# Moving a GpSimd share of the attention-to-FFN transition to VectorE, with a shorter bisection step

## What is computed

```python
x = x + jnp.tanh(g_xattn[0]) * _L0_xattn_ref(_layernorm(x), ctx_1024, ...)   # ends with gru_cell
x = x + jnp.tanh(g_ffn[0]) * _L0_ffn_ref(_layernorm(x), ...)

def _L0_ffn_ref(x, ...):
    scores = jax.nn.sigmoid(h @ gate_w.T)                     # 4096 x 16
    topk_score, topk_ids = jax.lax.top_k(scores.T, cap)       # 512 tokens for each of 16 experts
    xin = h[topk_ids]
    eo = jax.nn.silu(xin @ gw + gb) * (xin @ up + up_b)
    eo = eo @ down + down_b
    out = zeros.at[topk_ids].add(eo * topk_score)
    shared = (jax.nn.silu(x @ sh_gate_w.T) * (x @ sh_up_w.T)) @ sh_down_w.T
    return out + shared
```

## Time and profile before

| | us |
|---|---|
| median of three runs (lowest, highest) | 1204.84 (1204.55, 1205.53) |
| the profiled execution: its time | 1202.21 |
| the profiled execution: its span | 1200.5 |
| PE busy | 1114.3 (93%) |
| DVE busy | 820.7 (68%) |
| ACT busy | 559.2 (47%) |
| POOL busy | 436.6 (36%) |

### The profile page before, as it was taken

One profiled execution on the slowest core, in us unless ns is written; L12 is line 12 of the kernel. 1 busy time (PEld: TensorE's weight loads), 2 busy tenths in 40 slices (PEclk: granted clock), 3 DMA queues, 4 the chain that ended last, 5 costly groups with the idle time before them and its releaser, 6 DMA issues. The chain is left out here.

```text
span 1200.5 us, 18388 instructions
## 1 busy us (share of the span) xinstructions
PE 1114.3 (93%) x6174; PEld 964.1 (80%) x6174; DVE 820.7 (68%) x1552; ACT 559.2 (47%) x839; POOL 436.6 (36%) x334
## 2 busy tenths in 40 slices
PE   5659999999999787999988999999999999999996
PEld 3548888888888566888876888888888888888896
DVE  7575878787865986778864666566666665666663
ACT  4243545544546466232334554455555544555542
POOL 5232444344411733343541232243323423343332
PEclk9659999999999899999998999999999999999999
DMA  4310011010104234001045434454444334544421
GB/s 158 97 36 1 3 34 25 11 35 0 35 1 127 67 106 133 22 17 35 18 143 178 117 96 127 136 141 94 125 133 135 96 123 140 141 95 124 133 37 18
DMA packets 47525, 98.75 MB, mean 82 GB/s; under 512 B 11392, under 2 KB 37248, under 8 KB 43136
## 3 DMA queue, kind: packets, MB, share of 16 engines
q1 hardware_dynamic: 33728, 79.13, 20.4%
q0 software_dynamic: 12288, 17.31, 8.5%
q10 hardware_dynamic: 1472, 1.84, 0.4%
HBM read 74.11 MB, written 17.07 MB: 76 GB/s over the span
## 5 line engine op out<-in xcount | busy, mean ns | idle before, releaser
L2067 DVE SCALAR_TENSOR_TENSOR hid<-wide,b_up,silu 128x512 f32<-128x512 f32 x120 | 90.1, 751 | 165.8 <-PE wide L1317 159.4
L956 POOL DMA_INDIRECT out_tokens<-y,idx_out x64 | 111.8, 1747 | 235.2 <-DVE y L2049 188.7
L1317 PE MATMUL wide<-xt_hi,w_hi 128*128 128x512 f32 x480 | 189.3, 394 | 3.1 <-DVE xt_lo L2032 3.1
L1317 PE MATMUL wide<-xt_lo,w_hi 128*128 128x512 f32 x480 | 188.6, 393 | 0.0
L1317 PE MATMUL wide<-xt_hi,w_lo 128*128 128x512 f32 x480 | 187.6, 391 | 0.0
L1619 ACT ACTIVATE silu<-wide,b_gate 128x512 f32<-128x512 f32 x120 | 82.1, 685 | 147.8 <-PE wide L1317 147.8
L1331 PE MATMUL down<-w_hi,hid_hi 128*128 128x256 f32 x480 | 136.6, 284 | 0.0
L1331 PE MATMUL down<-w_lo,hid_hi 128*128 128x256 f32 x480 | 135.9, 283 | 0.0
L1331 PE MATMUL down<-w_hi,hid_lo 128*128 128x256 f32 x480 | 135.7, 283 | 0.0
L1628 ACT ACTIVATE hid_hi<-hid 128x512 fp32r<-128x512 f32 x120 | 76.0, 633 | 101.1 <-DVE hid L2067 101.1
L2017 DVE TENSOR_TENSOR w_lo<-raw,w_hi 128x768 fp32r<-128x768 f32 x128 | 121.4, 949 | 0.0
(11 more groups left out here) (320 smaller groups left out, 2516.2 us busy)
## 6 DMA issues: line engine op xcount, KB each, us to landing
raw<-in_w_expert SPq DMA_DIRECT2D x32, 1536.0 KB, 6.7
work<-in_x SPq DMA_DIRECT2D x8, 512.0 KB, 4.7
token_rows<-work SPq DMA_DIRECT2D x8, 512.0 KB, 3.2
out_tokens<-y SPq DMA_DIRECT2D x8, 512.0 KB, 3.0
attn<-rms_c SPq DMA_DIRECT2D x24, 128.0 KB, 2.3
attn<-expo SPq DMA_DIRECT2D x24, 128.0 KB, 2.4
b_down<-in_down_b SPq DMA_DIRECT2D x1, 2048.0 KB, 12.5
sh_full<-in_w_shared SPq DMA_DIRECT2D x1, 1536.0 KB, 6.1
```

Source lines behind the costliest of these rows:

```text
L956: pool.indirect_dma_start(out, bass.IndirectOffsetOnAxis(idx_out[:, j:j + 1], 0), y[:, j, :], None, compute_op=ALU.add).then_inc(g_add, 16)
L1317: last = nc.tensor.matmul(bank[:, f % 2, :], w[f // HALF_F][:, f % HALF_F, (c + k) * P:(c + k + 1) * P], x_[:, k, :], start=(m == 1), stop ...
L2067: nc.vector.scalar_tensor_tensor(hid[:, f % 2, :], eup[:, f % 2, :], b_up[:, bass.ds(e, 1), f:f + 1].rearrange("p a b -> p (a b)"), silu[: ...
```

## The change

1. VectorE adds x for all groups straight out of PSUM. `copy_x` on ScalarE and `add_x` on GpSimd go.
2. `h_full` goes: `high` on ScalarE rounds straight from PSUM, and VectorE makes all eight `slots_lo` from PSUM (`h_low`). PSUM banks are therefore held until VectorE has read them.
3. The four `chain` calls now take the groups (0, 1, 2), (3, 4), (5, 6) and (7). The order of steps on PE, ACT and DVE is rewritten; PE's first `into_hidden` now stands behind all eight routers.
4. The bisection keeps one value, `cand`, in place of `thr` and `bit`: two small instructions after each count in place of four. The constants come from 64 memsets of one column on GpSimd.
5. From slice 18 on VectorE makes `hid_lo` (`own_low`), and from group 4 on it adds the residual (`own_y`). GpSimd's loop ends after four groups.
6. Half of the writes of `token_ids` are issued by ScalarE's queue. The loads of `raw`'s second half and of `b_down`, issued ahead of the gather before, now wait for the gather to land.

GpSimd's transition work, VectorE's and ScalarE's in the diff:

```diff
-                add_x(0)
-                add_x(1)
-                add_x(2)
-                add_x(3)
+                for u in range(32):
+                    nc.gpsimd.memset(bit_f[:, u:u + 1], float(1 << (29 - u)) if u < 30 else 0.0)
+                    last = nc.gpsimd.memset(bit_i[:, u:u + 1], 1 << (28 - u) if u < 29 else 0)
+                last.then_inc(p_bit, 1)
...
-                h_low(0)
-                h_low(1)
-                h_low(2)
-                add_x(6)
-                h_low(3)
-                h_low(4)
-                h_low(5)
...
-                def copy_h(g):
+                def high(g):
 
                     act.wait_ge(t_h, g + 1)
-                    full = h_banks(g)[:, :, :]
-                    if g < SUB_POOL:
-                        full = h_full[:, :, group_of(g)]
-                        nc.scalar.activation(full, h_banks(g)[:, :, :], ACT.Copy).then_inc(a_hf, 1)
-                        act.wait_ge(a_hf, g + 1)
-                    nc.scalar.activation(slots_hi[:, :, group_of(g)], full, ACT.Copy).then_inc(a_hh, 1)
+                    nc.scalar.activation(slots_hi[:, :, group_of(g)], h_banks(g)[:, :, :], ACT.Copy).then_inc(a_hh, 1)
...
-                gru_unit(LAST, 1, 2, 1, None, (), (later(copy_h, 1), later(normalise_x1, 3)))
-                gru_unit(LAST, 1, 3, 0, None, (), (later(copy_h, 2),))
-                gru_unit(LAST, 1, 3, 1, later(copy_x, 6))
+                def steps(*todo):
+                    return tuple((lambda step=step, g=g: step(g)) for step, g in todo)
+
+                gru_unit(LAST, 1, 0, 0)
+                gru_unit(LAST, 1, 0, 1, None, steps((shared_hi, 0), (shared_hi, 1)))
+                gru_unit(LAST, 1, 1, 0, None, steps((shared_hi, 2), (shared_hi, 3)))
+                gru_unit(LAST, 1, 1, 1, None, (), steps((normalise_x1, 0)))
+                gru_unit(LAST, 1, 2, 0, None, steps((normalise_x1, 1)), steps((high, 0), (normalise_x1, 2)))
+                gru_unit(LAST, 1, 2, 1)
+                gru_unit(LAST, 1, 3, 0, None, (), steps((high, 1), (normalise_x1, 3)))
+                gru_unit(LAST, 1, 3, 1)
+                high(2)
+                normalise_x1(4)
+                high(3)
+                normalise_x1(5)
+                high(4)
+                normalise_x1(6)
+                high(5)
+                high(6)
                 nc.scalar.preload_act_table(ACT.Sigmoid)
-                copy_h(3)
-                normalise_x1(4)
-                normalise_x1(5)
-                copy_h(4)
-                copy_h(5)
-                normalise_x1(6)
```

PE's order and VectorE's:

```diff
-                turn_slots(5, (v_x1, 1))
-                turn_h(1, (a_hf, 1))
-                gru_unit(LAST, 1, 3, 0)
-                turn_h(2, (a_hf, 2))
-                gru_unit(LAST, 1, 3, 1, lambda: turn_slots(6, (v_x1, 2)))
-                turn_h(3, (a_xs, 5))
-                pe.wait_ge(p_sh, FS)
-                pe.wait_ge(a_r, RUN_UNITS + 1)
-                pe.wait_ge(a_z, RUN_UNITS + 1)
-                pe.wait_ge(*h_low_done(0))
-                into_hidden(0, 0, 0)
+                turn_slots(5, (v_x1, 5))
+                gru_unit(LAST, 1, 3, 0, lambda: turn_h(1, (v_hlo, 1)))
+
+                def middle():
+                    turn_slots(6, (v_x1, 6))
+                    turn_h(2, (v_hlo, 2))
+
+                gru_unit(LAST, 1, 3, 1, middle)
+                turn_h(3, (v_x1, 7))
                 pe.wait_ge(p_gw, 2)
+                pe.wait_ge(v_hlo, 3)
                 router(0)
                 router(1)
+                router(2)
                 turn_slots(7, (a_h, RUN_UNITS + 1), (v_pre, RUN_UNITS + 1))
-                router(2)
-                turn_h(4, (a_hf, 4))
+                turn_h(4, (v_hlo, 4))
                 router(3)
-                turn_h(5, (v_x1, 3))
+                turn_h(5, (a_r, RUN_UNITS + 1), (a_z, RUN_UNITS + 1))
+                turn_h(6, (v_hlo, 5))
+                turn_h(7, (v_x1, 8))
                 router(4)
                 router(5)
-                turn_h(6, (a_hf, 5))
-                turn_h(7, (a_hf, 6))
                 router(6)
                 router(7).then_inc(m_log, 1)
                 pe.wait_ge(p2, 3 + 2 * G)
+                pe.wait_ge(p_sh, FS)
+                into_hidden(0, 0, 0)
                 into_hidden(1, 0, 1)
...
-                gru_group(LAST, 1, 0, (lambda: first_x1(0, 1),), (lambda: first_x1(2, 3),))
-                gru_group(LAST, 1, 1, (lambda: chain(0),), (lambda: chain(1),))
-                gru_group(LAST, 1, 2, (lambda: first_x1(4),), (lambda: first_x1(5),))
-                gru_group(LAST, 1, 3, (lambda: chain(2),))
-                first_x1(6)
+                gru_group(LAST, 1, 0, (lambda: first_x1(0, 1),), (lambda: first_x1(2),))
+                gru_group(LAST, 1, 1, (lambda: first_x1(3), lambda: chain(0)))
+                def h_low(g):
+
+                    dve.wait_ge(a_hh, g + 1)
+                    nc.vector.tensor_tensor(slots_lo[:, :, group_of(g)], h_banks(g)[:, :, :],
+                                            slots_hi[:, :, group_of(g)].bitcast(F32), ALU.subtract).then_inc(v_hlo, 1)
+
+                gru_group(LAST, 1, 2, (lambda: first_x1(4), lambda: chain(1)), (lambda: h_low(0), lambda: first_x1(5)))
+                gru_group(LAST, 1, 3, (lambda: h_low(1), lambda: first_x1(6), lambda: chain(2)))
+                h_low(2)
                 first_x1(7)
+                h_low(3)
                 chain(3)
                 g = G - 1
-                dve.wait_ge(v_ln, G // 2)
+                dve.wait_ge(v_ln, len(CHAINS))
```

The bisection, the late slices and the issues of SP and ACT:

```diff
                 def bisect_keep(u):
 
+
                     dve.wait_ge(m_cnt, u + 1)
-                    nc.vector.tensor_scalar(keep[:, :], small[:, 0:1], float(CAP), -1.0, ALU.is_ge,
+                    nc.vector.tensor_scalar(keep[:, :], small[:, 0:1], float(CAP), bit_f[:, bass.ds(u, 1)], ALU.is_lt,
                                             ALU.mult).then_inc(v_bis, 1)
-                    dve.wait_ge(v_bis, 3 * u + 2)
-                    nc.vector.scalar_tensor_tensor(thr[:, :], keep[:, :], bit[:, 0:1], thr[:, :], ALU.bitwise_and,
-                                                   ALU.bitwise_or).then_inc(v_bis, 1)
-                    dve.wait_ge(v_bis, 3 * u + 3)
-                    nc.vector.tensor_scalar(bit[:, :], bit[:, :], 1, None, ALU.logical_shift_right).then_inc(v_bit, 1)
-                    dve.wait_ge(v_bit, u + 1)
-
-                def hidden(n, f):
+                    dve.wait_ge(v_bis, 2 * u + 1)
+                    nc.vector.scalar_tensor_tensor(cand[:, :], keep[:, :], bit_i[:, bass.ds(u, 1)], cand[:, :],
+                                                   ALU.bitwise_or, ALU.bitwise_xor).then_inc(v_bis, 1)
...
+                def own_low(n):
+                    dve.wait_ge(a_hid, n + 3)
+                    nc.vector.tensor_tensor(hid_lo[:, n % FS, :], hid[:, n % 2, :], hid_hi[:, n % FS, :].bitcast(F32),
+                                            ALU.subtract).then_inc(v_lo, 1)
+
+                def late_hidden(n):
+
+                    if n > OWN_LO:
+                        own_low(n - 1)
+                    hidden(n, n % FS, n < OWN_LO + 2)
+
+                def own_y(g):
+                    dve.wait_ge(a_y, g + 2)
+                    plus_x1(nc.vector, g)
...
-                for q in range(E // BLK):
+                for q in range(0, E // BLK, 2):
                     sp.dma_start(idv[:, :, q, :], ids_sb[:, q, :]).then_inc(w_ids, 16)
                 sp.wait_ge(w_ids, 16 * E // BLK)
                 sp.dma_start(idx_all[:, :, :], ids.rearrange("e (p j) -> p e j", j=BLK)).then_inc(l_idx, 16)
-                sp.wait_ge(m_ids, HALVES)
+                store_y(G - 2)
+                sp.wait_ge(g_in_, 16 * BLK)
                 sp.dma_start(raw[:, HALF_F:FE, :], w_expert[0, :, HALF_F:FE, :]).then_inc(l_w[1], 16)
                 sp.dma_start(b_down[:, :, :], down_b.rearrange("(a e) d -> a e d", a=1).to_broadcast([P, E, D]))\
-                    .then_inc(l_b, 16)
-                store_y(G - 2)
+                    .then_inc(l_bd, 16)
                 store_y(G - 1)
...
+                        if (g, f) == (G - 2, FS - 2):
+                            act.wait_ge(v_ids, 1)
+                            for q in range(1, E // BLK, 2):
+                                act.dma_start(idv[:, :, q, :], ids_sb[:, q, :]).then_inc(w_ids, 16)
```

More of the change, by code:

```diff
@@ L190, in flamingo_kernel @@
         rtmp2 = small_place("rtmp2", [P, G * BLK])
-        thr = small_place("thr", [P, 1], I32)
-        bit = small_place("bit", [P, 1], I32)
         cand = small_place("cand", [P, 1], I32)
@@ L1549, in scale_sums @@
                                          scale=tanh_g[:, 1:2]).then_inc(a_y, 1)
-                def later(step, g):
-                    return lambda: step(g)
                 act.sem_inc(a_silu, 2)
@@ L1831, in chain @@
                 def chain(q):
-                    own = slice(2 * q * BLK, 2 * (q + 1) * BLK)
```

(20 more changed lines are left out.)

155 lines of the change are left out of this document (66 added, 89 removed).

## The result

Timed in turn with the kernel before, the changed kernel takes 1207.05 us (median, 1204.56 to 1208.09), the kernel before 1204.35; the ratio is 1.0019, with a 95% interval from 1.0013 to 1.0026. The forecast was 1201.1 with a range from 1196 to 1206. The profiled execution took 1208.09 us, its span 1206.4.

What follows compares the result with a forecast made beforehand. TensorE was taken as the bound from 562 to 626.3 us, with transition, bisection and hand-over open. +6.0 - 2.2 - 7.5 = -3.7 us, so 1204.8 - 3.7 = 1201.1 us, range 1196 to 1206.

Steps and rivals of the forecast that it cites:

- Term 2: Bisection: VectorE's shorter chain after each count helps only where TensorE waits, at group turns; -2.2 us, between -1.0 and -4.0.
- Term 1: Transition: VectorE's added work delays the routers and idle TensorE falls to half clock; +6.0 us, bounds +2.2 and +12.
- Rival E: Transition: `sh_lo` holds four VectorE steps, 1.5 us each, plus another slow burst; 8 us more, 1209; chance 0.14.
- Rival C: Transition: TensorE's clock is low in every burst up to the last router; +3.2 us, 1204.3, no change; chance 0.12.
- Term 3: Late slices and hand-over: gather lands before TensorE ends the shared expert, expert 0 starts earlier; -7.5 us, bounds -5 and -8.
- Rival D: Hand-over: late `raw` load shares the DMAs with `b_down`, so TensorE stands 3 us in expert 0; 1204.1; chance 0.09.

Runs made afterwards that it cites:

- e1: Changed kernel with the bisection's keep value in a PSUM column, so that `cand` reads one SBUF tensor instead of two: 1195.08 us.
- e4: Changed kernel with the old bisection of the kernel before put back (four small instructions a count): 1199.09 us.
- e5: Kernel before with the bisection's keep value in a PSUM column, so that `thr` reads one SBUF tensor: 1200.40 us.
- e9: Changed kernel with keep in PSUM and each of GpSimd's four `sh_lo` instructions cut into four: 1194.65 us.
- e2: Changed kernel with VectorE's loop over the bisection's groups written out, so that no operand is addressed by a register: 1202.96 us.

## Why the prediction was wrong

**Term 2, the bisection, is the step that failed:** -2.2 forecast, +7.5 measured, and no bound on that side. "TensorE is the bound of a slice, so this counts only where it waits" took it that a shorter chain on VectorE can't hurt. I had the hold in hand in the same paragraph, for `thr` at a group's turn, and in the first term as a rule, but never laid the new `cand` against `hid_lo` inside a slice. It was placed by the two steps removed: VectorE runs ahead of TensorE, waits 0.4 us for the product, and its one instruction with two SBUF tensors lands on GpSimd's start. From then on a slice is a closed chain over four engines, `hid`, ScalarE's `hid_hi`, `hid_lo`, `cand`, count, product, keep, `cand`, count, `hid`. From one `hid` to the next in the trace: 1.44 to `cand` (498.92 to 500.36), 1.33 until its hold ends and the count starts (501.69), 1.33 for count and product (503.02), 0.60 from keep to the next count (503.62), 0.68 until `hid` starts behind it: 5.38 us, the slice. e1 and e4 show the cause, e5 that the same hold sat in the old kernel's group turns. The sign set for this term, waits for counts of 2 us or less, came out at 7.7. The registers, priced at 0.1 a count, cost 0.2 for the whole stage without the hold, and 5.6 with it.

The mechanism of the gain was right where nothing is held: e4 against e1, 82.2 to 78.6 us, though this takes the hold out of the group's turns too. Between e5 and e1, neither held, the new bisection brings 0.4 us. The -2.2 were thus the hold at the turns, not the shorter chain.

**Term 1, the transition:** +6.0 forecast, +5.7 measured. The steps are there: one wait of 9.2 us ahead of the first router ("issue" in the table; the low part of group 2 ends at 452.23, the router starts at 452.33), routers 0 to 2 in 6.20 us (5.9), the routers' end at 478.6, which is 476.7 on before's clock (476.7). The first router was 2.9 us later than I had it, as `sh_lo` held two steps by 3.1 us, one of the signs that I had named as wrong (steps of 2.7 us in 388 to 403). That the routers' end still fitted is luck, by offsetting errors: one of them is the turn of group 6, forecast at half clock (1.9) and run in 1.06, the rest I haven't parted. Rival E had this mechanism and the wrong price: e9 takes 2.5 us of the hold away and gains 0.3. Rival C, the low clock in later bursts, is what takes it back in e9, while in the changed kernel routers 4 to 7 ran at 1.00. The warning of the Trainium skill ("TensorE: Matmul & The Clock Gate", "HAM oscillation") fits e9 better than the kernel it was weighed for.

**Term 3, late slices and hand-over:** -7.5 forecast for both. The hand-over measured -7.8, the late slices -1.1, or +0.5 at the same clock (+0.3 forecast), so -7.3 where the clock is left out. The last part of the gather is issued at 636.3, 3.9 us ahead of TensorE's end at 640.15, and TensorE turns its rows without a wait; expert 0 starts 3.9 us behind that end (3.9). In the working, 612.1 + 0.6 + 1.9 is 614.6 and not 614.7, which changes nothing. No wait for `hid_lo` appears in the late slices, one of 0.4 for ScalarE's y. Rival D is out: ScalarE waits 3.9 us for `raw` until 646.1, but TensorE waits for nobody there, and the experts take 562.3 us against 562.5. `raw` is issued at 639.54 and has landed 6.6 us later (6.3).

**The sum:** -3.7 became +4.1 by the stages and +2.7 by the medians. Had Term 2 been right, 9.7 us less, the kernel would stand near 1197, inside the range; e4, which only takes its old form back, is at 1199.1. That is 4.7 below the kernel before, timed in turn with it, where Terms 1 and 3 alone had -1.5. By the stages, with the late slices taken at the same clock, e4 is 2.0 below (5.6 - 0.1 + 0.5 - 7.8 - 0.1, rounded), as the two terms have it; the 3 us more by the medians stay open.

## What to carry to other kernels

A shorter chain on an engine with slack isn't free if it moves an instruction: before removing a small step, look what each remaining two-tensor SBUF instruction of VectorE will run beside on GpSimd, above all in a loop, where a hold can close a ring over several engines and then decides every turn. One operand in PSUM frees such an instruction, at no cost here. And where one engine works through a slow burst, first issue what another engine is waiting for: here it was worth 6.4 us of transition, a second slow burst that went with it included, and filling the idle time 1.7.

## What the runs showed of the hardware

- A VectorE instruction of one element with two tensors in SBUF takes 0.22 us, or 1.30 when it starts with a GpSimd `tensor_tensor` of 1.29, or 1.60 inside one of 2.38; with one of the two in PSUM 0.22 at the same instant. The Trainium skill has the rule ("SBUF — State Buffer", "Who interferes with whom"): a VectorE instruction with two SBUF inputs contends with a GpSimd instruction that reads SBUF, for a whole instruction. The trace agrees, down to the hold ending with one GpSimd instruction (e9), and shows it for one element as for 1024. GpSimd is held in turn: a `sh_lo` of 1.82 us took 2.81. The count, of one input, took its 0.75 beside GpSimd in every run. The comparison for `tie`, also of one input but done in 0.48 us in e1, took 1.92 in e2, when GpSimd's addition to y (565.03 to 567.44) ran; in e1 that addition held the scan behind it, 3.31 us instead of 1.23. So an input count of one doesn't protect every instruction.
- An operand addressed by a register adds 0.09 us between two dependent VectorE instructions (0.34 against 0.25 from keep to `cand`), where I had 0.1 a count.
- The granted clock can take back on TensorE what VectorE gains: 2.7 of 2.9 us in e9.
